# Cross attention: tiles rearranged, probabilities times folded values in plain fp32 from single copies; segment memory kept as 64 columns per head

## What is computed

```python
# 1. segment attention: 16 heads of 64, segments of 128 tokens, a memory carried over the segments
sq  = elu(qs) + 1.0
mem = mem + einsum('bhsk,bhsv->bhkv', sq, vs)          # 64 x 64 per head
scores = einsum('bhsk,bhtk->bhst', qs, ks) * scale
att_dot = softmax(scores) @ vs
num = einsum('bhsk,bhkv->bhsv', sq, mem)
att = gate * (num / den) + (1.0 - gate) * att_dot       # then @ Wo
# 2. cross attention on the context: 16 heads of 64, 77 keys
q = query @ w_q;  k, v = split(context @ w_kv)
out = softmax(q @ k.T * SCALE) @ v                      # then @ w_out + b_out
# 3. a feed-forward part with attention over the query axis, two l2 norms and gelu
```

## Time and profile before

| | |
|---|---|
| three runs | 2028.80, 2031.43, 2032.51 us (median 2031.43) |
| the profiled execution | 2030.26 us, of which 2028.5 us are the span of the trace |
| mean granted TensorE clock | 0.978 of full speed |
| busy share of the span | PE 91%, DVE 74%, ACT 75%, POOL 27% |
| segment attention | from 0 to about 850 us |
| cross attention | its tiles from about 893 to 1222 us |
| the rest | from about 1225 us to the end |

### The profile page before, as it was taken

How to read it: one execution, slowest core, us unless ns; L and a number is a source line. 1 busy time by engine, 2 the same in 40 slices (tenths; PEclk the granted TensorE clock), 3 DMA queues, 4 the chain that set the end, 5 groups by cost and what they waited for, 6 DMA issues and landing times. The chain is left out here.

```text
span 2028.5 us, 43194 instructions
## 1 busy us (share of the span) xinstructions
PE 1844.1 (91%) x15254; PEld 1272.0 (63%) x15354; DVE 1508.8 (74%) x2893; ACT 1527.4 (75%) x4376; POOL 554.3 (27%) x659
## 2 busy tenths in 40 slices
PE   6999999999999999688888888899999999999986
PEld 5888888888888887568888887722222222222264
DVE  7777777777777776255555555599999999999935
ACT  6777777777777776257776764599999999999953
POOL 3344333333334444015564540000000000000023
PEclk9999999999999999899999998999999999999997
DMA  7223222233223233330101003933453343343001
GB/s 167 43 59 58 59 59 58 59 59 58 59 59 58 59 59 53 109 100 14 39 14 39 14 7 101 252 47 43 57 70 43 61 66 43 59 67 44 1 21 62
DMA packets 139646, 121.60 MB, mean 60 GB/s; under 512 B 78747, under 2 KB 111407, under 8 KB 139439
## 3 DMA queue, kind: packets, MB, share of 16 engines
q1 hardware_dynamic: 139439, 118.88, 29.5%
HBM read 77.29 MB, written 41.53 MB: 59 GB/s over the span
## 5 line engine op out<-in xcount | busy, mean ns | idle before, releaser
L1888 DVE TENSOR_REDUCE s_neg_max<-s_ring 128x1 f32<-128x1024 f32 x512 | 588.1, 1207 | 23.0 <-PE s_ring L1803 22.9
L1851 ACT ACTIVATE s_prob<-s_ring,s_neg_max 128x1024 f32<-128x1024 f32 x512 | 570.5, 1115 | 16.9 <-DVE s_neg_max L1888 16.8
L1816 PE MATMUL s_acc<-s_prob,s_v_norm 128*32 128x256 f32 x4096 | 327.9, 393 | 11.6 <-ACT f_zT_all L1843 10.3
L1803 PE MATMUL s_ring<-f_stack 128*128 128x512 bf16 x924 | 291.4, 389 | 34.1 <-issue 14.4
L1272 ACT ACTIVATE x_prob<-x_psum,x_neg_max 128x77 f32<-128x77 f32 x512 | 160.5, 333 | 92.9 <-DVE x_neg_max L1426 92.9
L489 ACT ACTIVATE a_prob<-a_psum,a_neg_max 128x128 f32<-128x128 f32 x512 | 179.9, 377 | 61.4 <-DVE a_neg_max L689 61.4
L1816 PEld LDWEIGHTS s_acc<-s_prob,s_v_norm 128*32 128x32 f32 x4096 | 81.5, 108 | 230.0 <-issue 215.4
L1803 PEld LDWEIGHTS s_ring<-f_stack 128*128 128x128 bf16 x1024 | 58.6, 97 | 244.5 <-ACT s_prob L1851 225.5
L1871 POOL TENSOR_TENSOR s_v_norm<-f_v_all,s_row_inv 128x64 f32<-128x64 f32 x128 | 37.6, 294 | 570.5 <-DVE s_row_inv L1881 570.5
L584 POOL TENSOR_SCALAR a_relu_ring<-a_qT 128x512 f32<-128x512 f32 x64 | 99.0, 1563 | 323.3 <-ACT a_qT L460 296.4
L38 PE MATMUL a_psum<-a_xT_hi,a_w_hi 128*128 128x256 f32 x512 | 153.1, 299 | 6.0 <-DVE a_w_lo L627 6.0
(11 more groups left out here) (200 smaller groups left out, 4246.3 us busy)
## 6 DMA issues: line engine op xcount, KB each, us to landing
f_stack<-qk_thirds SPq DMA_DIRECT2D x256, 128.0 KB, 6.1
segment_values<-a_v_stage SPq DMA_DIRECT2D x64, 256.0 KB
a_v_pos<-segment_values SPq DMA_DIRECT2D x512, 32.0 KB
qk_thirds<-p_third SPq DMA_DIRECT2D x16, 768.0 KB, 8.2
a_x_in<-in_x_dram SPq DMA_DIRECT2D x16, 256.0 KB, 3.2
a_x_res<-in_x_dram SPq DMA_DIRECT2D x32, 128.0 KB, 2.8
after_attention<-a_normed SPq DMA_DIRECT2D x32, 128.0 KB, 2.4
x_x_in<-after_attention SPq DMA_DIRECT2D x32, 128.0 KB, 2.0
```

The lines of the kernel that those rows point to most:

```text
L1803: last = pe.matmul(ring[n % 3][:, f * HALF:(f + 1) * HALF], k_stack[:, slot, j, kt * P:(kt + 1) * P], q_stack[:, slot, j, f * HALF:(f + 1) ...
L1816: last = pe.matmul(acc[32 * j:32 * j + 32, s], v_norm[:, step // KT % 2, step % 4, j, :], prob[:, step % 4, j, s], start=step % (2 * KT) = ...
L1851: act.activation(prob[:, step % 4, j, :], ring[n % 3][:, :], ACT.Exp, bias=neg_max[:, step % 2, j:j + 1], accum_out=row_sum[:, step % 2, j ...
L1888: dve.tensor_reduce(neg_max[:, step % 2, j:j + 1], ring[n % 3][:, :], AX_X, ALU.max, negate=True).then_inc(max_ready, 1)
```

## The change

In the segment attention `mem` becomes 64 columns wide per head. `memory` makes eight matmuls of M = 64, N = 64 per unit, in pairs to the PSUM partitions 0 to 63 and 64 to 127, in place of four of M = 128, N = 128; `attend` makes eight of K = 64, M = 64, N = 128 with `mem`, in pairs on opposite quadrants of the array, in place of four of K = 128, M = 128, N = 128. DVE adds both heads of a pair in one op of 128 partitions. The zeroing of `mem` goes.

In the cross attention the transposed probabilities and u are single plain fp32 copies. `attend` makes one plain fp32 matmul per chunk in place of three fp32r ones; `low_probT`, `low_first_u`, `high_u` and `low_u` go, and with them the buffer `u_in`: u of a batch is loaded by DMA straight into `u_even` or `u_odd`. The order of the tile loop changes on ACT, DVE and POOL; PE's order stays.

```diff
-        mem = sb("mem", [P, 2, GR, P])
+        mem = sb("mem", [P, 2, GR, DH])
...
                 for gi in range(4):
-                    last = pe.matmul(LATE_BANK[half][:, gi * P:(gi + 1) * P], phi_tok[:, u, gi * P:(gi + 1) * P],
-                                     v_pos[:, it % 2, t, half * 4 + gi::GR, :], start=True, stop=True)
+                    for e in range(2):
+                        at = gi * P + e * DH
+                        last = pe.matmul(LATE_BANK[half][rows(e), gi * DH:(gi + 1) * DH], phi_tok[:, u, at:at + DH],
+                                         v_pos[:, it % 2, t, e * GR + half * 4 + gi, :], start=True, stop=True)
...
-                    last = pe.matmul(NUM_BANK[:, gi * P:(gi + 1) * P], mem[:, t, g, :], phiT[:, t, g, :],
-                                     start=True, stop=True)
+                    for e in range(2):
+                        last = pe.matmul(NUM_BANK[rows(e), gi * P:(gi + 1) * P], mem[rows(e), t, g, :],
+                                         phiT[rows(e), t, g, :], start=True, stop=True)
...
-                for e in range(2):
-                    out = mem[rows(e), t, groups, rows(e)]
-                    product = LATE_BANK[half][rows(e), :].rearrange("p (g k) -> p g k", k=P)[:, :, rows(e)]
...
+                out = mem[:, t, groups, :]
+                product = LATE_BANK[half][:, 0:4 * DH].rearrange("p (g k) -> p g k", k=DH)
...
-        u_in = sb("u_in", [P, CHUNKS, D])
-        u_even = sb("u_even", [P, 2, CHUNKS, D], F32R)
+        u_even = sb("u_even", [P, CHUNKS, D])
+        u_rest = sb("u_rest", [P, 2, 2, 2, D])
...
+            sp.wait_ge(first_taken, FIRST)
+            sp.wait_ge(u_padded, 1)
             operands(1)
...
-                        sp.wait_ge(u_high, b * U_PIECES)
-                        sp.wait_ge(u_low, b * U_PIECES)
+                        sp.wait_ge(y_done, b * PER_BATCH)
                         operands(b + 1)
...
                     if t > 0 and t % PER_BATCH == 0:
-                        pe.wait_ge(u_high, b * U_PIECES)
-                        pe.wait_ge(u_low, b * U_PIECES)
+                        pe.wait_ge(u_landed, b * 32)
                 for chunk in range(*TURNS[k]):
-                    left = probT_hi[:, chunk, :], probT_lo[:, chunk, :]
-                    right = u_hi[b % 2][:, chunk, :], u_lo[b % 2][:, chunk, :]
-                    for n, (i, j) in enumerate(((0, 0), (0, 1), (1, 0))):
-                        last = pe.matmul(Y_BANK[:, 0:D], left[i], right[j], start=chunk == 0 and n == 0,
-                                         stop=chunk == CHUNKS - 1 and n == 2, skip_group_check=True)
+                    last = pe.matmul(Y_BANK[:, 0:D], probT[:, chunk, :], u[b % 2][:, chunk, :], start=chunk == 0,
+                                     stop=chunk == CHUNKS - 1, skip_group_check=True)
...
@@ POOL, tile loop
-            for t in range(TILES):
...
+            for t in range(TILES + 3):
+                if t >= 3:
+                    root(t - 3)
+                if 1 <= t <= TILES:
+                    normalise_and_split(t - 1, 2)
+                    normalise_and_split(t - 1, 3)
+                if t < TILES:
+                    normalise_and_split(t, 0)
+                    normalise_and_split(t, 1)
+                    add_bias(t)
...
@@ DVE, before the tile loop
-            low_first_u(4)
+            dve.wait_ge(first_taken, FIRST)
+            dve.memset(u_odd[:, CHUNKS - 1, :], 0.0).then_inc(u_padded, 1)
```

158 lines of the change are left out of this document (49 added, 109 removed).

## The result

The changed kernel takes 1981.19 us (median of four runs, 1979.85 to 1982.43), the kernel before 2031.26 in the same comparison (four runs, 2028.80 to 2032.51). The ratio is 0.9755, with a 95% interval from 0.9738 to 0.9772: faster by 2.4%. The forecast was 1977 us with a range from 1964 to 1997. The profiled execution took 1982.07 us, 1980.3 of them the span: 48.2 less than the 2028.5 of before.

What follows compares the result with a forecast made beforehand. PE was taken as the bound, in the cross attention with a wait for `low_probT`. Cross attention -37.5 and memory step -17 made -54.5 us from 2030.26: 1975.8, as a median 1977 us, range 1964 to 1997.

Steps and rivals of the forecast that it cites:

- the case that it put first: Whole kernel: cross attention -37.5 us and segment memory step -17 us, giving 1977 us; chance 0.58.
- The product: Cross attention tiles: ten plain matmuls replace 30 fp32r, the wait goes, step 10.15 to 8.96 us; -34.5 us over 29 steps.
- The mean step of 10.15: Cross attention: mean time per tile over 29 steps, taken as PE's work of 8.33 us plus 1.81 of waits and gaps.
- the split of u: Cross attention: it vanishes from ACT and POOL, which are not the bound; booked as nothing.
- The new orders: Cross attention tile loop: ACT copies ahead of the third group's exps; about 3 us of slack left, no wait.
- Edges: Cross attention's start and its drain of the last two tiles: -1.5 us each.
- Memory step: Segment attention: units at 0.55 us, fewer DVE sums, PE then waiting for `residual`; 1.15 us per iteration, -17 us in 16.
- Rival 1: Segment attention: memory units stay at 1.0 us, gaining only 6 us there; 1988 us, chance 0.20.
- Attend: Segment attention: eight matmuls on opposite quadrants cost +0.0 per unit; 0 us over 64 units, from -9 to +63.
- Rival 2: Cross attention tile: a wait returns through ACT's new order or a batch start, step 9.6; 1995 us, chance 0.15.
- Rival 3: Segment attend: quadrant pairs do not overlap, units 1.98 us, deciding above 1.67; slower at 2051 us, chance 0.05.
- Rival 4: Cross attention: PE's clock falls; at half clock throughout, the kernel about 200 us slower; chance 0.02.

Runs made afterwards that it cites:

- half_product: The changed kernel with every second chunk of the cross attention's product left out (5 of 10 matmuls per tile): 1922.36 us, one execution.
- seg_only: The kernel before with only the segment attention's change, cross attention as before: 2017.66 us, ratio 0.9939.
- cross_only: The kernel before with only the cross attention's change, segment attention as before: 1994.57 us, ratio 0.9821.
- spread_longer_by_160: The changed kernel with POOL spreading `mem` into 128x128 blocks for the old segment attend, plus 80 unused matmuls on PE: 1975.84 us, ratio 0.9728.

## Why the prediction was right, and where its terms were off

The forecast of 1977 us stands against 1981.2, 4 us off a change of 50, and the case that it put first came true in both stages. The mechanism was right: PE alone sets the tile once the subtraction is gone, and the memory step of the segment stage shortens by its units and DVE's sums. But the total is better than its terms, since some of them were off in opposite directions. By its steps:

- **The product.** Ten plain matmuls of 0.433 cost 4.33 as worked out from the earlier trace rows; the wait of 36.1 us went and none came back. The step is 9.02, forecast 8.96. The difference lies in a turn: followed by a plain fp32 attend it takes 0.44 (950.20 to 950.64), not the 0.36 that I took for both turns of four from the earlier trace rows. Over 29 steps -32.9 instead of -34.5.
- **The mean step of 10.15** was right as a sum, but I read it as one kind of step. A step without a split was 9.62, so the chain for `low_probT` explains 0.60 per step, 17.4 us. I booked nothing for the split of u, "which are not the bound", and nothing for the batch starts. Yet the steps with them held 6.9 and 8.0 us of the gain: in six of the twelve with a split PE waited a second time for `low_probT`, 0.26 to 0.31 us, and at a batch start also for `residual` and for POOL's part of g, some 0.6 us each. The mean carried these costs into the sum, though the reasoning had priced them at nothing: that the total fits is luck to this extent. The new orders on ACT, DVE and POOL, which I costed at nothing, are worth 4 us, at the first step and the batch starts.
- **Edges.** Start -2.4, forecast -1.5; drain -1.4, forecast -1.5.
- **Memory step.** 1.15 forecast, 1.21 measured: units at 0.54 (forecast 0.55) and an idle of 0.87 before the third. `residual` was not what PE waited for behind them, as I had named for a sign: it ended at 540.74, and PE started L325 at 540.97 without a noted wait. Rival 1 is out.
- **Attend.** This term was mis-sized: "+0.0 per unit" from the earlier trace rows was +0.12 to +0.13, some 8 us in 64 units, 0.04 of it in the unit and 0.09 in the step ahead of it. The nearest row gave the unit almost right (1.02), but its predecessor had to be read as well. So a steady iteration is 0.75 us shorter (49.98 to 49.23) and not the 1.1 that I had named as the sign: 12 us in all instead of 17. That the profiled segment stage gained 15.3 is chance for the larger part of the difference, the 2.7 us at half the clock in the last iteration of before.
- **Rival 2** did not come: L1152 has no wait for ACT, every step is 9.02, and half_product shows at least 2 us of room.
- **Rival 3**, slower through the quadrants, had its price wrong as well: with neighbours in one quadrant, at 0.19 us per matmul, a unit takes 1.5 and not 1.98, so this rival would not have reached its own point of 1.67.
- **Rival 4**, the clock, did not come either: it is at 1.00 in all the tiles of the changed kernel. The three falls to 0.50 in the kernel before, at the batch starts, are gone, but they had cost nothing: seg_only has the same tile code and no such fall, and its two steps around a batch start take 12.05 + 9.80 = 21.85 us, against 13.19 + 8.68 = 21.87.
- **Outside the change** I booked nothing, and the later stages took 3.1 us more: 1.5 in the query softmax, by its loop, and 1.8 at the end. The latter is in this page as a matmul group partly at a clock of 0.50 (3.4 us of it); cross_only and most others do not have it, spread_longer_by_160 has the same row. Its cause is open. Timeline of PE after the change:

```profile
1884.47 5.40 PE L1914 MATMUL g_z<-f_zT_all,f_w_out 128*128 128x512 f32 x8 [2.15 <-ACT g_square L1952]
```

The same group before the change:

```profile
1934.47 3.70 PE L1970 MATMUL g_z<-f_zT_all,f_w_out 128*128 128x512 f32 x8 [2.15 <-ACT g_square L2008]
```

## What to carry to other kernels

Price a stage that waits on a chain as PE's own work from start to start, and the gain of cutting the chain is the step minus that work; here it held to 0.06 us. Look at the single steps before you take their mean for a steady one: what the mean holds besides the chain may be worth as much. When a matmul changes its tile shape, measure the start of the instruction ahead of it too, since here 0.09 of 0.13 us was paid there. Before crediting or blaming an edit with the last few microseconds, compare the stages that it does not touch: instructions added ahead of a loop moved one of them by up to 10 us.

## What was unexpected of the hardware

- The cost of going round a loop on PE depends on the length of the program ahead of it: 610.0 to 620.5 us for the same stage, in two turns of the loop, and in fourteen profiles grouped by the number of PE's records ahead of it, modulo 256.
- A matmul of 64x64 weights and 128 columns in plain fp32 takes 0.19 us when its neighbours lie in the same quadrant (1.50 for eight), 0.13 when they lie in the opposite one (1.02 for eight), against 0.25 for one of 128x128 (0.99 for four).
- The first matmul on a quadrant behind an item of 128x128 weights starts 0.09 us later than a full one would (0.53 instead of 0.44 behind a turn). Behind the memory units in column pairs the transpositions took 0.85 instead of 0.79 us.
